# Tanh in place of SiLU in the routed expert tiles of a gated two-layer block, with ScalarE's order of work rewritten

## The chip, the cores and the metric

One core of a Trainium2 chip runs the whole program. The metric is the device time of one execution in microseconds (us). In what follows PE is TensorE, ACT is ScalarE, DVE is VectorE, POOL is GpSimd and SP is SyncE, which issues most of the DMA transfers.

## The reference

Two layers work on a residual stream `x` of 4 x 512 tokens with 512 channels, in fp32. Each layer adds a state-space block that reads a context (and is gated by `silu(layernorm(x))`), and then a feed-forward block. Layer 0's feed-forward block is a mixture of 16 experts, four of them chosen for each token, plus a shared expert. The part that the change touches is the experts' hidden layer:

```python
def body(acc, inp):
    g, u, d, we = inp
    y = jax.nn.silu(x @ g.T) * (x @ u.T) @ d.T
    return (acc + we[:, None] * y, None)
out, _ = jax.lax.scan(body, jnp.zeros_like(x), (gate_proj, up_proj, down_proj, cw.T))
```

`silu(a)` is `a * sigmoid(a)`, which is `0.5 * a * (1 + tanh(a / 2))`. The state-space block runs this recurrence over 512 time steps, for 512 channels with 16 states each:

```python
dA = jnp.exp(d_t[..., None] * A)
state = state * dA + (d_t * u_t)[..., None] * B_t[:, None, :]
y_t = jnp.einsum('ben,bn->be', state, C_t)
```

## The kernel before

The state-space blocks of the two layers and four sequences are eight stages `s` = 0 to 7. A stage has 32 units (16 states times two halves of the channels). For each unit ACT computes the decays, two activations with `Exp` (`decay`, L712); DVE multiplies `du` by the row of B (`mul_b`, L1702) and runs the scan (`scan`, L1710); POOL multiplies by the row of C (`mul_c`, L457), and the result is added up.

Stages 5 to 7 (`FIRST_B` is 5) run together with the routed experts of layer 0. The token rows are sorted by expert into 47 tiles: 32 whole ones of 256 rows and 15 half ones of 128 rows. From tile 4 on every third one is a half tile. Each of the 48 turns (16 in each of the three stages) holds two units of the recurrence and, in all but the first, one tile `j`. The engines walk the same turns, each in its own order written out by hand (`tile_turn` in each engine's block), and meet by semaphores.

For one tile PE transposes the gathered rows (`tile_transposes`, L1164), ACT copies them from PSUM to SBUF (`tile_rows`, L762), and PE multiplies them by the gate and up weights (`tile_in`, L1185), in two parts `it` = 0 and 1 that each end in one PSUM bank, `GU(j, it)`: the gate in its first half, the up product in its second. ACT applies the gate's function (`tile_silu`, L769), DVE multiplies by the up product (`tile_hidden`, L1728), and PE multiplies by the down weights (`tile_out`, L1196). ACT copies the result out (`tile_out`, L776) and SP stores it (`store_tile`, L341). The transposes of tile `j+1` are written into the banks of tile `j`'s gate and up products and so wait for its `tile_hidden`.

The weights of a tile are 1.5 MB and go into one of two slots (`load_tile_w`, L335). The load for tile `j+2` waits until PE is done with tile `j` (`y_done`). SP also loads, in each turn, a pair of B and C rows (`load_pair`, L316), which waits for POOL's `mulc_done`.

In 12 or so turns of stages 5 and 6 the engines also prepare the next stage (`prep`): PE's input projection (`in_one`, L1027), its projections L1058 and L1078, DVE's convolution (L1427), ACT's `conv_tap_one`, `silu_one` (which stays SiLU), `step_abs_one`, `exp_half`, `log_half` and so on.

Before the change ACT's order in a turn is: first decay of the turn, `tile_silu(j, 0)`, `tile_out(j - 1)`, `tile_silu(j, 1)`, `tile_rows(j + 1, 0)`, `tile_rows(j + 1, 1)`, second decay. DVE's order is: `tile_hidden(j, 0)`, `add_y`, `mul_b`, `tile_hidden(j, 1)`, `scan`, then `add_y`, `mul_b`, `scan` for the second unit, and the preparing work.

`ACT_TABLE_LOAD` rows are put ahead of an activation by the compiler where the function needs another table than the one loaded.

Of the kernel before, what the change touches and what calls it, by code (L numbers as in the profile page):

```python
# [69 lines left out]
def build(nc, t):  # L70
    with ExitStack() as ctx:
# [137 lines left out]
        y_done, yev, dve_step = sem("y_done"), sem("yev"), sem("dve_step")  # L209
# [326 lines left out]
        def _(act):  # L536
# [227 lines left out]
            def tile_silu(j, it):  # L764
                act.wait_ge(gu_done, j * 2 + it + 1)
                if j >= 2:
                    act.wait_ge(y_done, DONE[j - 1])
                n = P * BLOCKS[j]
                nc.scalar.activation(HT[:, j % 2, it, 0:n], GU(j, it)[:, 0:n], ACT.Silu).then_inc(sil_ready, 1)  # L769
# [141 lines left out]
            def tile_turn(s, i, prep):  # L911
                p = s + 1
                for u in range(BODY):
                    n = i * BODY + u
                    j = TPS * (s - FIRST_B) + n - 1
                    decay(s, i, 2 * u)
                    if prep:
                        if 2 <= n < 2 + ET:
                            conv_tap_one(p, n - 2)
                        if n == 10:  # L920
                            exp_half(p, 0)
                        if n == 13:
                            log_half(p, 0)

                    if j >= 0:
                        tile_silu(j, 0)
                    if j >= 1:
                        tile_out(j - 1)
                    if prep:
                        if n == 7:  # L930
                            x_dbl(p)
                        if n == 12:
                            plus_half(p, 1)
                        if n in (8, 9):
                            step_abs_one(p, 2 * (n - 8))
                    if j >= 0:
                        tile_silu(j, 1)
                    if prep and 3 <= n < 3 + ET:
                        silu_one(p, n - 3)
                    if 0 <= j < NTILE - 1:  # L940
                        tile_rows(j + 1, 0)
                    if prep:
                        if n == 11:
                            plus_half(p, 0)
                        if n in (8, 9):
                            step_abs_one(p, 2 * (n - 8) + 1)
                        if n == 14:
                            seed_half(p, 0)
                        if n == 15:
                            seed_half(p, 1)  # L950
                    if 0 <= j < NTILE - 1:
                        tile_rows(j + 1, 1)
                    decay(s, i, 2 * u + 1)
                    if s == FIRST_B and n == 0:
                        act.wait_ge(w_free, HS * FIRST_B + PRE_W)
                        nc.scalar.activation(flat(Y[:, 0, 2:4]), flat(PS[:, 0:2]), ACT.Copy).then_inc(y4_ready, 1)
                    if prep:
                        if n == 10:
                            exp_half(p, 1)
                        if n == 13:  # L960
                            log_half(p, 1)
# [5 lines left out]
            tile_out(NTILE - 1)  # L967
# [425 lines left out]
        def _(dve):  # L1393
# [130 lines left out]
            def route(b0, b1, work, rank1, rank2):  # L1524
# [59 lines left out]

                link(nc.vector.tensor_scalar(tot, tot, 2 * SCALING, TG[:, 2:3], ALU.mult, ALU.mult))
# [137 lines left out]
            def tile_hidden(j, it):  # L1723
# [3 lines left out]
                dve.wait_ge(sil_ready, j * 2 + it + 1)  # L1727
                nc.vector.tensor_tensor(h, h, GU(j, it)[:, TILE:TILE + n], ALU.mult).then_inc(h_ready, 1)  # L1728
# [362 lines left out]
```

## Time and profile before

| what | us |
|---|---|
| median of 3 runs | 1503.17 |
| lowest and highest run | 1501.42, 1510.47 |
| the profiled execution (its time) | 1501.42 |
| the profiled execution's span | 1499.7 |
| the stretch of the 47 expert tiles, from 788 to 1325 | 537.0 |

The span is the time from the first to the last instruction of the profiled execution; some 1.7 us of its time lie outside. The experts' tiles take 36% of it. Everything that the change touches lies in this stretch, apart from one constant in the routing.

### The profile page before, as it was taken

How to read it: one execution, taken by the hardware profiler on the slowest of the kernel's cores; microseconds unless marked ns; L12 is line 12 of the kernel's file. 1: busy time of each engine (PE TensorE's matmuls, PEld its weight loads, DVE VectorE, ACT ScalarE, POOL GpSimd, SP SyncE). 2: the span in 40 equal slices, each digit the busy share in tenths (PEclk: the TensorE clock that was granted, in tenths of full speed). 3: DMA queues.
4: the chain of work that ended last, by engine and by line, in shares of the span. 5: the costliest groups of instructions: out<-in, count | busy, mean ns of one | idle time of the engine just before them, and what ended most of it. 6: DMA issues, size and time to landing. Idle time of an engine off the chain costs nothing. (4 is left out here: it accounts for less than half of the span.)

```text
span 1499.7 us, 14543 instructions
## 1 busy us (share of the span) xinstructions
PE 1261.5 (84%) x4518; PEld 721.7 (48%) x4518; DVE 1353.0 (90%) x1319; ACT 971.4 (65%) x1528; POOL 784.2 (52%) x411
## 2 busy tenths in 40 slices
PE   7785796899699868996989998899988899826998
PEld 3331242443244324442556666566666666615555
DVE  4999999998999899988898988999899999888894
ACT  5766568575864666625866788767887767734442
POOL 0465566545555553550465555555565665565632
PEclk9799999999999998998899999999999999977999
DMA  7444545535544443450356678677777887755531
GB/s 254 109 141 127 126 141 142 154 98 151 133 146 124 127 127 109 126 154 2 99 181 233 239 260 291 230 272 239 254 275 230 286 273 273 270 183 147 167 100 57
DMA packets 99837, 264.31 MB, mean 176 GB/s; under 512 B 10832, under 2 KB 11344, under 8 KB 93616
## 3 DMA queue, kind: packets, MB, share of 16 engines
q1 hardware_dynamic: 87936, 225.36, 48.4%
q0 software_dynamic: 11440, 37.50, 7.7%
q8 instruction: 36, 0.59, 0.2%
q10 hardware_dynamic: 384, 0.52, 0.1%
q14 instruction: 41, 0.34, 0.1%
HBM read 233.73 MB, written 29.62 MB: 176 GB/s over the span
## 5 line engine op out<-in xcount | busy, mean ns | idle before, releaser
L457 POOL TENSOR_TENSOR state<-state,bc_rows 128x1024 f32<-128x1024 f32 x254 | 599.2, 2359 | 613.6 <-DVE banks L1702 613.5
L1095 PE MATMUL banks<-state,ident 128*128 128x512 f32 x640 | 323.7, 638 | 106.6 <-POOL state L457 106.6
L1710 DVE TENSOR_TENSOR_SCAN state<-decay,banks 128x1024 f32<-128x1024 f32 x176 | 402.0, 2284 | 11.4 <-DVE banks L1702 5.0
L1702 DVE TENSOR_TENSOR banks<-du,bc_rows 128x1024 f32<-128x1024 f32 x256 | 314.5, 1229 | 13.4 <-DVE state L1710 0.5
L1185 PE MATMUL banks<-z_gate,expert_w 128*128 128x256 f32 (+1 forms) x1504 | 284.1, 347 | 7.5 <-DMA expert_w<-in_moe_w 7.5
L1185 PEld LDWEIGHTS banks<-z_gate,expert_w 128*128 128x128 f32 x1504 | 248.8, 191 | 60.1 <-issue 18.9
L1095 PEld LDWEIGHTS banks<-state,ident 128*128 128x128 f32 x640 | 118.0, 197 | 282.0 <-POOL state L457 170.0
L712 ACT ACTIVATE decay<-delta,neg_a 128x511 f32<-128x511 f32 x352 | 226.4, 710 | 16.8 <-DVE state L1710 11.6
L1710 DVE TENSOR_TENSOR_SCAN state<-expert_w,banks 128x1024 f32<-128x1024 f32 x80 | 182.9, 2286 | 6.9 <-ACT expert_w L712 4.2
L1196 PE MATMUL banks<-expert_w,hidden 128*128 128x512 f32 x316 | 156.2, 610 | 2.3 <-ACT expert_out L776 1.2
L1721 DVE TENSOR_TENSOR y_scan<-y_scan,state 128x1024 f32<-128x1024 f32 x94 | 114.3, 1216 | 3.6 <-POOL state L457 2.0
L712 ACT ACTIVATE expert_w<-delta,neg_a 128x511 f32<-128x511 f32 x160 | 104.1, 711 | 8.5 <-DVE state L1710 6.9
L762 ACT ACTIVATE z_gate<-banks 128x512 f32<-128x512 f32 (+1 forms) x94 | 49.6, 529 | 76.1 <-PE banks L1164 75.5
L712 ACT ACT_TABLE_LOAD x65 | 83.4, 1283 | 1.6 <-ACT x_dbl L578 0.4
L769 ACT ACTIVATE hidden<-banks 128x256 f32<-128x256 f32 (+1 forms) x94 | 33.2, 353 | 61.3 <-PE banks L1185 60.8
L1196 PEld LDWEIGHTS banks<-expert_w,hidden 128*128 128x128 f32 x316 | 54.8, 198 | 34.5 <-issue 31.2
L1728 DVE TENSOR_TENSOR hidden<-hidden,banks 128x256 f32<-128x256 f32 (+1 forms) x94 | 35.1, 373 | 32.6 <-ACT hidden L769 31.9
L1144 PE MATMUL banks<-y_scan,expert_w 128*128 128x512 f32 x128 | 59.0, 615 | 5.0 <-DVE hidden L1736 5.0
L769 ACT ACT_TABLE_LOAD x47 | 60.3, 1283 | 0.8
L1046 PE MATMUL banks<-ones,ident 128*128 128x128 f32 x274 | 36.1, 290 | 28.4 <-DVE neg_mean_rstd L1933 28.4
L1353 PE MATMUL banks<-expert_w,du 128*128 128x512 f32 x128 | 55.6, 592 | 0.0
L1016 PE MATMUL banks<-ctx_t,in_w 128*128 128x512 f32 x96 | 47.3, 641 | 9.6 <-DMA ctx_t<-in_ctxT 7.3
(318 smaller groups left out, 1659.2 us busy)
## 6 DMA issues: line engine op xcount, KB each, us to landing
bc_rows<-bc_d SPq DMA_DIRECT2D x208, 512.0 KB
expert_w<-in_moe_w SPq DMA_DIRECT2D x48, 1536.0 KB, 9.1
ys_d<-expert_out SPq DMA_DIRECT2D x32, 512.0 KB, 5.4
ctx_t<-in_ctxT SPq DMA_DIRECT2D x8, 512.0 KB, 6.7
x_res<-in_x SPq DMA_DIRECT2D x4, 1024.0 KB, 10.7
xn_d<-y_scan SPq DMA_DIRECT2D x4, 1024.0 KB, 7.7
ys_d<-expert_out SPq DMA_DIRECT2D x15, 256.0 KB, 5.9
out_x<-x_res SPq DMA_DIRECT2D x3, 1024.0 KB, 6.0
```

The source lines that it names most:

```text
L457: nc.gpsimd.tensor_tensor(W[:, c % 4], W[:, c % 4], bcast2(BC[:, u, 1, :]), ALU.mult).then_inc(mulc_done, 1)
L712: ins = nc.scalar.activation(DAS[c % n][:, m, 1:], DEL[:, s % 2, et, 1:], ACT.Exp, scale=AN[:, lay(s), et, state:state + 1])
L762: nc.scalar.activation(XST[:, 2 * h:2 * h + 2, 0:n], XT(j)[:, h, :, 0:n], ACT.Copy).then_inc(xst_ready, 1)
L769: nc.scalar.activation(HT[:, j % 2, it, 0:n], GU(j, it)[:, 0:n], ACT.Silu).then_inc(sil_ready, 1)
L1095: mm = nc.tensor.matmul(PS[:, m], ID[:, :], W[:, c % 4, m, :], start=False, stop=True, skip_group_check=True)
L1144: mm = nc.tensor.matmul(AUX[g], MW[:, 0, at:at + P], XNT[:, k, :], start=(k == 0), stop=(k == ET - 1))
L1185: mm = nc.tensor.matmul(GU(j, it)[:, g * TILE:g * TILE + n], MW[:, u % 2, at:at + P], XST[:, k, 0:n], start=(k == 0), stop=(k == ET - 1))
L1196: mm = nc.tensor.matmul(out_bank(j, r), HT[:, u % 2, it, r * P:(r + 1) * P], MW[:, u % 2, at:at + D], start=(it == 0), stop=(it == IT - 1))
L1353: nc.tensor.matmul(PS[:, q], xnt[:, q, k * P:(k + 1) * P], BW[:, k, :], start=(k == 0), stop=(k == ET - 1))
L1702: nc.vector.tensor_tensor(drive(s), DU[:, s % 2, 2 * h:2 * h + 2, :], bcast2(BC[:, u, 0, :]), ALU.mult).then_inc(mulb_done, 1)
L1710: nc.vector.tensor_tensor_scan(flat(W[:, c % 4]), flat(DAS[c % da_slots(s, i)]), flat(drive(s)), 0.0, ALU.mult, ALU.add).then_inc(scan_don ...
L1721: nc.vector.tensor_tensor(y, y, W[:, k % 4], ALU.add).then_inc(w_free, 1)
```

## The change

The routed experts take `Tanh` with a scale of 0.5 in place of `Silu` (`tile_silu` becomes `tile_tanh`). DVE's `tile_hidden` gets one more instruction ahead of its product, `(tanh + 1) * gate`, which reads the gate from PSUM and writes to the same place in SBUF as before; a new semaphore `hg_ready` orders the two. What DVE has then is twice the SiLU product, and the routing weights are scaled by `SCALING` where it was `2 * SCALING` (the gate factor in `TG[:, 2:3]` holds a half already, which the shared expert, whose hidden layer is computed with `Tanh` before and after, needs).

ACT's order in a turn becomes: first decay, `tile_tanh(j, 0)`, second decay, `tile_tanh(j, 1)`, `tile_rows(j + 1, 0)`, `tile_rows(j + 1, 1)`, `tile_out(j)`. So the output of tile `j` is copied out at the end of its own turn, not in the next. The preparing work is spread anew between them: `silu_one`, for one, stood behind `tile_silu(j, 1)` and stands now between the second decay and `tile_tanh(j, 1)`. PE, POOL and SP keep their orders.

```diff
--- before.py
+++ after.py
@@ -206,7 +206,7 @@
 
         xt_done, xst_ready, gu_done, sil_ready, h_ready = (
             sem("xt_done"), sem("xst_ready"), sem("gu_done"), sem("sil_ready"), sem("h_ready"))
-        y_done, yev, dve_step = sem("y_done"), sem("yev"), sem("dve_step")
+        hg_ready, y_done, yev, dve_step = sem("hg_ready"), sem("y_done"), sem("yev"), sem("dve_step")
 
         rows_var, rows_std, rows_zn, rows_z = sem("rows_var"), sem("rows_std"), sem("rows_zn"), sem("rows_z")
         combined, exp_ready, shift_ready = sem("combined"), sem("exp_ready"), sem("shift_ready")
@@ -761,12 +761,12 @@
                 n = P * BLOCKS[j]
                 nc.scalar.activation(XST[:, 2 * h:2 * h + 2, 0:n], XT(j)[:, h, :, 0:n], ACT.Copy).then_inc(xst_ready, 1)
 
-            def tile_silu(j, it):
+            def tile_tanh(j, it):
                 act.wait_ge(gu_done, j * 2 + it + 1)
                 if j >= 2:
                     act.wait_ge(y_done, DONE[j - 1])
                 n = P * BLOCKS[j]
-                nc.scalar.activation(HT[:, j % 2, it, 0:n], GU(j, it)[:, 0:n], ACT.Silu).then_inc(sil_ready, 1)
+                nc.scalar.activation(HT[:, j % 2, it, 0:n], GU(j, it)[:, 0:n], ACT.Tanh, scale=0.5).then_inc(sil_ready, 1)
 
             def tile_out(j):
                 if j:
@@ -917,54 +917,51 @@
                     if prep:
                         if 2 <= n < 2 + ET:
                             conv_tap_one(p, n - 2)
-                        if n == 10:
-                            exp_half(p, 0)
-                        if n == 13:
-                            log_half(p, 0)
-
-                    if j >= 0:
-                        tile_silu(j, 0)
-                    if j >= 1:
-                        tile_out(j - 1)
-                    if prep:
                         if n == 7:
                             x_dbl(p)
                         if n == 12:
                             plus_half(p, 1)
-                        if n in (8, 9):
-                            step_abs_one(p, 2 * (n - 8))
                     if j >= 0:
-                        tile_silu(j, 1)
-                    if prep and 3 <= n < 3 + ET:
-                        silu_one(p, n - 3)
-                    if 0 <= j < NTILE - 1:
-                        tile_rows(j + 1, 0)
-                    if prep:
-                        if n == 11:
-                            plus_half(p, 0)
-                        if n in (8, 9):
-                            step_abs_one(p, 2 * (n - 8) + 1)
-                        if n == 14:
-                            seed_half(p, 0)
-                        if n == 15:
-                            seed_half(p, 1)
-                    if 0 <= j < NTILE - 1:
-                        tile_rows(j + 1, 1)
+                        tile_tanh(j, 0)
                     decay(s, i, 2 * u + 1)
                     if s == FIRST_B and n == 0:
                         act.wait_ge(w_free, HS * FIRST_B + PRE_W)
                         nc.scalar.activation(flat(Y[:, 0, 2:4]), flat(PS[:, 0:2]), ACT.Copy).then_inc(y4_ready, 1)
                     if prep:
+                        if 3 <= n < 3 + ET:
+                            silu_one(p, n - 3)
+                        if n in (8, 9):
+                            step_abs_one(p, 2 * (n - 8))
+                        if n == 10:
+                            exp_half(p, 0)
+                        if n == 11:
+                            plus_half(p, 0)
+                    if j >= 0:
+                        tile_tanh(j, 1)
+                    if 0 <= j < NTILE - 1:
+                        tile_rows(j + 1, 0)
+                    if prep:
+                        if n in (8, 9):
+                            step_abs_one(p, 2 * (n - 8) + 1)
                         if n == 10:
                             exp_half(p, 1)
                         if n == 13:
-                            log_half(p, 1)
+                            log_half(p, 0)
+                        if n == 15:
+                            seed_half(p, 1)
+                    if 0 <= j < NTILE - 1:
+                        tile_rows(j + 1, 1)
+                    if j >= 0:
+                        tile_out(j)
+                    if prep and n == 13:
+                        log_half(p, 1)
+                    if prep and n == 14:
+                        seed_half(p, 0)
 
             for s in range(FIRST_B, STAGES):
                 act.wait_ge(delta_ready, 2 * (s + 1))
                 for i in range(TURNS):
                     tile_turn(s, i, s + 1 < STAGES)
-            tile_out(NTILE - 1)
 
             act.wait_ge(ld_ffn1, 16 * 4)
             nc.scalar.activation(BB, BB, ACT.Copy, scale=TG[:, 3:4]).then_inc(bias_ready, 1)
@@ -1581,8 +1578,7 @@
                 link(nc.vector.reduce_sum(tot, cw, AX.X))
                 link(nc.vector.tensor_scalar(tot, tot, 1e-20, None, ALU.add))
                 link(nc.vector.reciprocal(tot, tot))
-
-                link(nc.vector.tensor_scalar(tot, tot, 2 * SCALING, TG[:, 2:3], ALU.mult, ALU.mult))
+                link(nc.vector.tensor_scalar(tot, tot, SCALING, TG[:, 2:3], ALU.mult, ALU.mult))
                 nc.vector.tensor_tensor(cw, cw, tot.unsqueeze(2).to_broadcast([P, nq, NE]), ALU.mult).then_inc(ranked, b1 - b0)
 
             def slots():
@@ -1725,6 +1721,9 @@
                 n = P * BLOCKS[j]
                 h = HT[:, j % 2, it, 0:n]
                 dve.wait_ge(sil_ready, j * 2 + it + 1)
+                nc.vector.scalar_tensor_tensor(out=h, in0=h, scalar=1.0, in1=GU(j, it)[:, 0:n], op0=ALU.add,
+                                               op1=ALU.mult).then_inc(hg_ready, 1)
+                dve.wait_ge(hg_ready, j * 2 + it + 1)
                 nc.vector.tensor_tensor(h, h, GU(j, it)[:, TILE:TILE + n], ALU.mult).then_inc(h_ready, 1)
 
             def shared_hidden(b, it):
```

## Rows read from the trace of the kernel before

**Rows 1.** The page: busy time of each engine over the whole span.

```profile
PE 1261.5 (84%) x4518; PEld 721.7 (48%) x4518; DVE 1353.0 (90%) x1319; ACT 971.4 (65%) x1528; POOL 784.2 (52%) x411
```

**Rows 2.** Windows, the expert-tile stage: busy time per engine, clock, DMA share, GB/s.

```profile
788.00:1325.00 537.00, 489.19 (x2186) 348.35 (x2184) 493.97 (x417) 400.56 (x606) 308.21 (x169) 0.98 0.75 255
```

**Rows 3.** Waits of DVE in that stretch: total us, times, longest.

```profile
DVE hidden L1728 <- ACT hidden L769: 31.9, 43, 2.1
DVE state L1710 <- DVE banks L1702: 5.0, 8, 0.6
```

**Rows 4.** Groups by line and shape, DVE, that stretch: busy, mean ns, idle before.

```profile
L1728 DVE TENSOR_TENSOR hidden<-hidden,banks 128x256 f32<-128x256 f32 x64 | 26.7, 417 | 26.6 <-ACT hidden L769 25.9
L1728 DVE TENSOR_TENSOR hidden<-hidden,banks 128x128 f32<-128x128 f32 x30 | 8.4, 281 | 6.0 <-ACT hidden L769 6.0
...
L1427 DVE SCALAR_TENSOR_TENSOR du<-banks,chan,du 128x511 f32<-128x511 f32 x8 | 5.8, 725 | 0.0
```

**Rows 5.** Groups by line, ACT, that stretch.

```profile
L712 ACT ACT_TABLE_LOAD x49 | 62.9, 1283 | 0.9
L769 ACT ACT_TABLE_LOAD x47 | 60.3, 1283 | 0.8
```

**Rows 6.** Timeline of ACT at a shared expert: start, duration, instruction.

```profile
294.51 0.60 ACT L755 ACTIVATE hidden<-banks 128x512 f32<-128x512 f32 x1 [2.30 <-PE banks L1144]
295.01 1.32 ACT L712 ACTIVATE expert_w<-delta,neg_a 128x511 f32<-128x511 f32 x2
```

**Rows 7.** Timeline of DVE at a shared expert.

```profile
700.68 0.69 DVE L1734 SCALAR_TENSOR_TENSOR hidden<-hidden,banks 128x512 f32<-128x512 f32 x1
701.41 0.69 DVE L1736 TENSOR_TENSOR hidden<-hidden,banks 128x512 f32<-128x512 f32 x1
```

**Rows 8.** Timeline across two turns, tile 45 (whole) to tile 46 (half).

```profile
1313.96 0.42 DVE L1728 TENSOR_TENSOR hidden<-hidden,banks 128x256 f32<-128x256 f32 x1
...
1314.30 2.28 DVE L1710 TENSOR_TENSOR_SCAN state<-decay,banks 128x1024 f32<-128x1024 f32 x1
...
1317.22 3.73 PE L1185 MATMUL banks<-z_gate,expert_w 128*128 128x128 f32 x32
...
1317.40 2.56 ACT L712 ACTIVATE decay<-delta,neg_a 128x511 f32<-128x511 f32 x4
...
1318.88 2.29 DVE L1710 TENSOR_TENSOR_SCAN state<-decay,banks 128x1024 f32<-128x1024 f32 x1
...
1319.98 1.28 ACT L769 ACT_TABLE_LOAD   x1
1321.27 0.28 ACT L769 ACTIVATE hidden<-banks 128x128 f32<-128x128 f32 x1
...
1321.58 0.29 DVE L1728 TENSOR_TENSOR hidden<-hidden,banks 128x128 f32<-128x128 f32 x1 [0.42 <-ACT hidden L769]
```

**Rows 9.** Chain that ended last, a whole tile: start, duration, instructions.

```profile
988.23 1.72 PE banks L1027 x4
...
1058.38 1.91 PE banks L1078 x4
...
1165.57 6.91 PE banks L1185 x32
1172.47 0.44 PE banks L1164 x4
1172.91 1.72 PE banks L1196 x4
```

**Rows 10.** The same chain where weights came last.

```profile
1230.54 11.89 DMA expert_w<-in_moe_w
...
1283.07 1.73 PE banks L1196 x4
1285.51 9.57 DMA expert_w<-in_moe_w
```

**Rows 11.** Timeline of the DMA issues on SP, the store behind that load.

```profile
1289.95 0.36 SPq L341 DMA_DIRECT2D ys_d<-expert_out  x1
```

## The prediction

> **What bounds the kernel now.** The page is read first: DVE is busy for 90% of the span, more than any other engine [rows 1]. The edits all act in the stretch of the expert tiles, so the windows view of that stretch is read next: of 537.0 us DVE is busy 494.0, PE 489.2 and ACT 400.6, at a granted clock of 0.98, and the DMA engines have a share of 0.75 [rows 2]. Two engines stand above 90%, and what matters is DVE's idle time, 537.0 - 494.0 = 43.0 us. The waits view says what ended it: 31.9 us, in 43 cases, by the activation that `tile_hidden` waits for (L769), and 5.0 us ahead of a scan [rows 3]. About 6 us more are spread.
>
> The timeline shows one such wait from end to end [rows 8]. DVE ends the product of tile 45 at 1314.38 (1313.96 + 0.42) and goes on without a stop to 1321.17, the end of the second scan, 6.8 us later. Meanwhile ACT runs four decays behind one table load (from 1317.40, 2.56 us), loads the other table (1319.98) and only then applies SiLU, at 1321.27. Its input had been there for some time: the PE began the gate and up products at 1317.22, and the first half of 3.73 us ends at 1319.1. DVE starts at 1321.58, with 0.42 us of idle time. So this wait is ACT's, and of table loads. Others are PE's, above all where it has extra work.
>
> **What the change removes.** SiLU and Exp alternate in every turn, at two table loads a turn: 49 ahead of decays and 47 ahead of SiLU, 123.2 us of ACT [rows 5]. With Tanh they go, if Tanh and Exp share a table. The trace bears that out: at a shared expert a Tanh at 294.51 is followed by decays at 295.01 with no load between [rows 6]. What stays in the stretch is the eight `silu_one`, with a load on each side (16 loads, 20.5 us), and about four for the logarithm. ACT falls from 400.6 us to about 400.6 - 123.2 + 20.5 = 298, 56% of the stretch. All of this lies on an engine with idle time; it is worth only what DVE and PE waited for it, at most 31.9 + 5.0 us.
>
> The page "ScalarE: Activation LUTs" of the Trainium skill (its section "What ACT_TABLE_LOAD costs") gives a switch as 1.283 us for the load and 1.38 us more to drain, 2.66 in all. The trace has only the first part: the load at 1319.98 ends at 1321.26 and the activation starts at 1321.27 [rows 8]. With the page's figure, as an estimate, the 96 loads would be worth 132 us more of ACT, and ACT would be as full as DVE.
>
> **What it adds.** DVE gets 94 instructions, 64 on 256 columns and 30 on 128. This instruction stands in the trace at the shared experts, on 512 columns: 0.69 us, and the product that waits for it starts 0.04 us after its end (700.68 + 0.69 = 701.37, next at 701.41) and takes 0.69 too [rows 7]. So it costs what the product costs, plus 0.04. The product takes 417 ns on 256 columns and 281 on 128 [rows 4]: 64 x 0.457 + 30 x 0.321 = 38.9 us. From below: an instruction that nothing waits for overlaps the next by 0.08 us (the scan at 1314.30 begins before 1314.38 [rows 8]); were that so here, 64 x 0.34 + 30 x 0.20 = 28 us. From above: the convolution's instruction of the same kind takes 725 ns on 511 columns [rows 4], 5% over 0.69, which gives about 41 us. I take 38.9, as the kind, the source bank and the wait are the same.
>
> All of it is on DVE, and nothing hides it but idle time. Where DVE no longer waits, one start in 43 cases moves back into the overlap: 43 x 0.08 = 3.4 us back. DVE's busy time becomes 494.0 + 38.9 - 3.4 = 529.5 us. With no idle time at all the stretch would shrink by 7.5 us; before, 43.0 were idle.
>
> **What idle time is left.** From the end of a tile's product (call it D) DVE reaches the next `tile_hidden` after 6.8 us. PE has then to do: the transposes and down products of the second half, 0.44 + 1.72 us, and half of the 6.91 us of the next gate and up products [rows 9] (the two rows of 0.44 and 1.72 come twice for a tile); a Tanh needs about 0.5 with its start. That is D + 0.05 + 2.16 + 3.46 + 0.5 = 6.2, so 0.6 us before it is wanted. A whole turn costs PE 6.91 + 2 x 2.16 = 11.2 us. For DVE, the 6.8 us hold two scans of 2.2 (each less its overlap) and `add_y` and `mul_b` once, so these take 2.4; its turn was 6.8 + 0.34 + 2.4 + 0.42, about 9.9, and becomes 10.8. A half tile costs PE about 6 (3.73 for the gate and up products [rows 8] and two halves of 2.16), and DVE 10.2. PE falls back by half a us in each of two whole tiles, and catches up in the half one. On plain turns DVE should not wait. The places where it should:
> - PE's extra work behind a whole tile where DVE has none: 1.72 us for an input projection, 1.91 for two of the other [rows 9]. Then the activation is at D + 8.1 against 6.8 and the second half late by 0.3: about 1.6 us each, at tiles 0, 5 and 23, together 5.
> - `silu_one` between the second decay and the second Tanh: two decays 1.4, load 1.3, SiLU 0.6, load 1.3 and the Tanh make the second Tanh late by about 0.7 in four or five of eight turns: 3. The mere order costs this; without it, nothing.
> - Weights. The load for tile j+2 is issued 0.7 us after PE's last product (1283.07 + 1.73, then 1285.51) and takes 9.57 there [rows 10]. For the whole tile behind a half one the chain is D + 2.2, 0.5 of PE's lag, 0.7, 9.6, 3.5, 0.5 = 17.0 us; DVE comes after 6.8 + 3.4 + 6.8 = 17.0, the middle term being its two products and what lies between them on a half tile (0.3 + 2.4 + 0.7). It is even at 9.6 us per load; some take 11.89 [rows 10]. I take 2 us over the 14 such places.
> - Starts and rests, POOL's lateness: 2 to 4.
>
> Together 13 us, give or take 5. The copy-out at the end of ACT's turn waits for PE (its end is D + 2.2), and behind it wait the next decay, which is ready by D + 4.4, and the Tanh, due at D + 5.7; the scan that needs the decay comes after two products, beyond D + 10. So this new wait costs nothing while PE keeps within 2 us or so of DVE, and if PE is later, DVE waits for PE anyway. SP's store of tile j-1 blocks `load_pair` for less time than before.
>
> **Sum.** 529.5 + 13 = 542.5 against 537.0: 5.5 us longer. Nothing else in the 1501.42 us of the profiled execution changes; one constant has the same price. That makes 1507. The median of the three runs lies 1.75 us above that execution, no more than runs differ by. I say 1506.
>
> **Rivals.**
> 1. *Balance* (the forecast): the loads' relief and DVE's new work are of one size. 1498 to 1514. For it: 38.9 us against 31.9 + 5.0 of waits. Against it: both are sums of small terms. Chance 0.70.
> 2. *All waits were ACT's.* If idle time falls to 4 us, 529.5 + 4 is 3.5 us less than 537.0, 1498; at the lower price of the instruction (28) it is 1487. For it: in rows 8 PE's result waited two us for ACT. Against it: PE's 11.2 us per whole tile and its extra work don't depend on ACT. (The switch of 2.66 us in the Trainium skill's page "ScalarE: Activation LUTs", section "What ACT_TABLE_LOAD costs", would end here: with it ACT would have set all 43 us.) Chance 0.15, of which 0.04 below 1488.
> 3. *The weights take over (slower).* The store of a tile is now issued right behind the load of the next weights, where before it came 4.4 us later (1285.51, then 1289.95) [rows 10, 11], and the rows for the transposes are gathered at the same time. If a load then lasts 11.9 us and not 9.6, each of the 14 whole tiles behind a half one is 2.3 us late: 32 us, 1538; it passes 1% at about 10.4 us per load, since 14 x 0.8 = 11 on top of the sum. For it: the 0.75 of DMA share and loads of 11.89 today. Against it: the bytes are the same, and the slower turns of DVE give the load more room. Chance 0.11.
> 4. *The rewritten order of ACT hurts elsewhere:* `x_dbl` and `plus_half` ahead of the first Tanh, the logarithm between the two `tile_rows`. They add 0.6 to 2.3 us each in some eight turns where ACT has over 1.5 us of room; if all of that lands on DVE, 10 us: 1517 or a bit more. Chance 0.04.
>
> **How the numbers follow.** Faster by over 1% is below 1488, slower by over 1% above 1518; about this much a measurement of this kernel can tell from no change. Faster: the 0.04 of rival 2. Slower: rival 3, half of rival 4 and 0.02 for the forecast's own terms being all too small, 0.15. Within 1%: 0.81. The range runs from 1494 (rival 2 with some idle time left) to 1520 (rival 3 at 10.5 us a load).
>
> **What the profile after would show.** Right: no table load at the decays of plain turns and some 20 in the stretch; ACT near 300 us there; DVE near 529 busy, the new instruction at 0.41 us on 256 columns with 0.04 to the product; DVE's waits for the Tanh below 12 us and at tiles 1, 6 and 24 or in the `silu_one` turns; loads of weights near 9.6. Wrong: loads over 10.4 us and PE's waits for `expert_w` grown (rival 3), DVE's idle time below 6 us (rival 2), or long waits at the turns of the logarithm (rival 4). The forecast falls if the added instruction is cheaper than 0.35 us, or if DVE's other instructions change their durations.

## The result and the profile after

The changed kernel takes 1515.38 us in the median of 8 runs (1514.14 to 1520.49), the kernel before, run beside it, 1508.26 us (1501.42 to 1513.34). The ratio is 1.0064, with a 95% interval of 1.0041 to 1.0087: the change costs some 10 us, and the table loads that it removes don't pay for it.

The two profiled executions differ by more, 1518.8 to 1499.7 us of span: the one before was the fastest of its eight runs, the one after 5 us slower than its median. The windows view of both, cut at the two ends of the expert tiles, tells where (columns: us; busy time and instructions of PE, weight loads, DVE, ACT, POOL; granted clock; DMA share; GB/s). Before, then after:

```profile
0.00:788.00 788.00, 645.12 (x1742) 290.83 (x1743) 723.86 (x624) 508.90 (x837) 385.61 (x174) 0.94 0.47 132
788.00:1325.00 537.00, 489.19 (x2186) 348.35 (x2184) 493.97 (x417) 400.56 (x606) 308.21 (x169) 0.98 0.75 255
1325.00:1499.70 174.70, 127.19 (x594) 82.52 (x592) 135.20 (x280) 61.99 (x86) 90.34 (x69) 0.89 0.44 133
```

```profile
0.00:796.87 796.87, 654.45 (x1742) 295.71 (x1743) 724.03 (x624) 508.94 (x837) 385.57 (x174) 0.94 0.49 131
796.87:1343.90 547.03, 489.87 (x2186) 346.87 (x2184) 525.42 (x511) 301.30 (x526) 312.57 (x169) 0.98 0.76 251
1343.90:1518.80 174.90, 127.20 (x594) 82.55 (x592) 135.16 (x280) 61.64 (x85) 89.86 (x69) 0.89 0.44 133
```

In the first stretch nothing of the program was changed and all engines but PE are busy for the same time, yet it lasts 788.0 us in one execution and 796.9 in the other. The kernels below show the same scatter: their first `tile_hidden` comes between 793.4 and 802.3 us. So each kernel is judged by its timed ratio, and the profiles by the stretch from the first start of `tile_hidden` to the last, which leaves the scatter ahead of it out. It is **530.7 us before and 540.6 after** (from starts read to 0.1 us), 9.9 us more, and the ratio says 9.7. Both measures have an error: the interval of a ratio is 3 to 4 us to either side, and a stretch is that of one execution. In some kernels below they differ by up to 6 us, and no run shows why; where it matters both are given.

Within the stage, ACT's groups by line after the change, which answer to [rows 5]:

```profile
L769 ACT ACTIVATE hidden<-banks 128x256 f32<-128x256 f32 (+1 forms) x94 | 32.4, 344 | 64.0 <-PE banks L1182 63.9
L712 ACT ACT_TABLE_LOAD x10 | 12.8, 1283 | 0.2
L571 ACT ACT_TABLE_LOAD x8 | 10.3, 1283 | 0.1
...
L627 ACT ACT_TABLE_LOAD x2 | 2.6, 1283 | 0.0
```

Of the 96 loads of [rows 5] 10 are left ahead of decays; with `silu_one` (L571) and the logarithm (L627) there are 20. ACT is busy 301.3 us where it was 400.6. DVE's groups by shape, which answer to [rows 4]:

```profile
L1727 DVE TENSOR_TENSOR hidden<-hidden,banks 128x256 f32<-128x256 f32 x64 | 26.9, 421 | 2.2
L1724 DVE SCALAR_TENSOR_TENSOR hidden<-hidden,banks 128x256 f32<-128x256 f32 x64 | 26.5, 414 | 12.3 <-ACT hidden L769 11.0 <-issue 0.9
L1727 DVE TENSOR_TENSOR hidden<-hidden,banks 128x128 f32<-128x128 f32 x30 | 8.6, 287 | 1.0
L1724 DVE SCALAR_TENSOR_TENSOR hidden<-hidden,banks 128x128 f32<-128x128 f32 x30 | 8.3, 275 | 0.2 <-ACT hidden L769 0.2
```

The new instruction (L1724) takes 414 and 275 ns, the product (L1727) 421 and 287. DVE is busy 525.4 us of 547.0 now, 494.0 of 537.0 before: 31 us more, and its idle time has halved, from 43.0 to 21.6. The waits view of the stage, which answers to [rows 3]:

```profile
ACT expert_out L776 <- DMA ys_d<-expert_out: 54.8, 28, 4.2
...
ACT decay L712 <- DVE state L1706: 33.6, 29, 3.2
...
ACT expert_out L776 <- PE banks L1193: 11.9, 33, 1.3
DVE hidden L1724 <- ACT hidden L769: 11.2, 21, 2.2
...
PE banks L1182 <- DMA expert_w<-in_moe_w: 6.7, 6, 1.7
...
DVE y_scan L1717 <- POOL state L457: 3.6, 7, 0.5
```

DVE's waits for the activation fell from 31.9 to 11.2 us. At the top ACT itself waits in two new ways: 54.8 us for the store of the tile before, and 33.6 for a scan. For the first the DMA view shows when the stores land (columns: KB of one transfer, median us from issue to landing); before, then after:

```profile
expert_w<-in_moe_w SPq DMA_DIRECT2D x45, 1536.0 KB, 9.1
...
ys_d<-expert_out SPq DMA_DIRECT2D x32, 512.0 KB, 5.4
```

```profile
expert_w<-in_moe_w SPq DMA_DIRECT2D x45, 1536.0 KB, 9.1
...
ys_d<-expert_out SPq DMA_DIRECT2D x32, 512.0 KB, 10.2
```

The store of a tile is issued right behind a load of weights (by 0.4 to 2.4 us in all turns but two, before by 3.8 to 8.3 in all but one) and lands after 10.2 us, where it took 5.4. The loads of weights have kept their 9.1. That it is the load ahead which delays the store is shown by a run below, `after_half_weights`: with the store as close behind a load of half the size, ACT's wait for it falls from 54.8 to 3.9 us.

### The profile page after: what moved, and what is told of

Read it like the earlier page. It is cut to its first block, busy times and chain, and to the rows that moved or that the text cites. A ratio compares the mean times of both kernels' runs of the same rounds, so it can differ in the third digit from the quotient of the medians.

```text
span 1518.8 us, 14557 instructions
## 1 busy us (share of the span) xinstructions
PE 1271.5 (84%) x4518; PEld 725.1 (48%) x4518; DVE 1384.6 (91%) x1413; ACT 871.9 (57%) x1448; POOL 788.0 (52%) x411
## 4 chain that ended last, share of the span: by engine, by line
DVE 35%; PE 30%; issue 8%; DMA 6%; POOL 5%; ACT 3%; DVEq 0%; SPq 0%; another core or an unknown queue 0%; ACTq 0%; POOLq 0%
DVE state L1706 15%; DVE banks L1698 10%; PE banks L1182 8%; PE banks L1092 5%; PE banks L1193 3%; DMA expert_w<-in_moe_w 3%; PE banks L1141 2%; DVE y_scan L1717 2%; POOL state L457 2%; PE banks L1036 2%; PE banks L1149 2%; DMA ys_d<-expert_out 1%; PE banks L1013 1%; DVE du L1424 1%; DVE hidden L1724 1%
## 5 line engine op out<-in xcount | busy, mean ns | idle before, releaser
L1092 PE MATMUL banks<-state,ident 128*128 128x512 f32 x640 | 328.3, 645 | 107.9 <-POOL state L457 107.6
L1706 DVE TENSOR_TENSOR_SCAN state<-decay,banks 128x1024 f32<-128x1024 f32 x176 | 402.1, 2285 | 10.2 <-ACT decay L712 5.8
L712 ACT ACTIVATE decay<-delta,neg_a 128x511 f32<-128x511 f32 x352 | 230.5, 712 | 48.5 <-DVE state L1706 43.7
L1717 DVE TENSOR_TENSOR y_scan<-y_scan,state 128x1024 f32<-128x1024 f32 x94 | 114.0, 1212 | 3.6 <-POOL state L457 3.6
L776 ACT ACTIVATE expert_out<-banks 128x512 f32<-128x512 f32 x79 | 45.5, 596 | 69.7 <-DMA ys_d<-expert_out 54.8
L472 POOL DMA_INDIRECT z_gate<-xn_d,selected x40 | 50.7, 1269 | 8.4 <-issue 5.3
L1043 PEld LDWEIGHTS banks<-ones,ident 128*128 128x128 f32 x274 | 35.2, 205 | 36.5 <-issue 36.5
## 6 DMA issues: line engine op xcount, KB each, us to landing
ys_d<-expert_out SPq DMA_DIRECT2D x32, 512.0 KB, 10.2
x_res<-in_x SPq DMA_DIRECT2D x4, 1024.0 KB, 10.8
```

Of the source, the lines that this page charges most:

```text
L712: ins = nc.scalar.activation(DAS[c % n][:, m, 1:], DEL[:, s % 2, et, 1:], ACT.Exp, scale=AN[:, lay(s), et, state:state + 1])
L1043: nc.tensor.matmul(bank[:, 0:P], ID[:, :], ON[:, :], start=True, stop=True)
L1092: mm = nc.tensor.matmul(PS[:, m], ID[:, :], W[:, c % 4, m, :], start=False, stop=True, skip_group_check=True)
L1706: nc.vector.tensor_tensor_scan(flat(W[:, c % 4]), flat(DAS[c % da_slots(s, i)]), flat(drive(s)), 0.0, ALU.mult, ALU.add).then_inc(scan_don ...
L1717: nc.vector.tensor_tensor(y, y, W[:, k % 4], ALU.add).then_inc(w_free, 1)
```

## Experiments

In the tables below "stretch" is the one just defined, from each kernel's profile; the last column is the time of three plain turns (a whole tile behind a half one, a whole one, a half one), the sum of the mean turn of each kind from the starts of the product in `tile_hidden` for tiles 32 to 45, where nothing is prepared. Ratios are to the kernel before, with their 95% intervals; "us by the ratio" is the ratio less 1, times 1508.26.

### Table loads and DVE's instruction taken apart

| kernel | table loads | DVE's instruction | ratio | us by the ratio | stretch | three turns |
|---|---|---|---|---|---|---|
| before | yes | no | 1 | 0 | 530.7 | 32.16 |
| `tanh_only` | no | no | 0.9939 (0.9919 to 0.9960) | -9.2 | 526.5 | 32.21 |
| `product_only` | yes | yes | 1.0117 (1.0096 to 1.0137) | +17.6 | 546.9 | 32.48 |
| `tanh_old_order` | no | yes | 1.0056 (1.0033 to 1.0080) | +8.4 | 540.7 | 32.69 |
| after | no | yes, new order | 1.0064 (1.0041 to 1.0087) | +9.7 | 540.6 | 32.73 |
| `after_no_product` | no | no, new order | 0.9961 (0.9937 to 0.9984) | -5.9 | 523.8 | 32.06 |

The expectations of this group count the stretch from the first to the last product of PE, on which the kernel before has 528.2 us and the changed one 537.6: some 3 us less than in the table.

**`tanh_only`.** One word changed in the kernel before:

```diff
-ACT.Silu).then_inc(sil_ready, 1)
+ACT.Tanh, scale=0.5).then_inc(sil_ready, 1)
```

> The kernel before with Tanh (scale 0.5) in place of Silu and nothing else: no factor gate*(1+..) on DVE, so the routed experts' values are not the reference's. It takes away the table loads alone. Theory A (whole tiles are set by PE's 11.2 us a turn, half tiles by DVE): the waits of DVE for the activation (31.9 us) mostly turn into waits for PE, so only about 10 us are gained: ratio 0.993, the stretch from the first to the last expert product 528.2 -> about 518 us. Rival B (the table loads were all that DVE waited for): -30 us, ratio 0.980, stretch 498.

The ratio is theory A's (9.2 us); of the stretch only 4.2 us came off, less than A's 10, and 3.3 of them before tile 15, where the next stage is prepared: three plain turns are no faster than before. Rival B is out. Its waits say why:

```profile
ACT hidden L769 <- PE banks L1185: 151.3, 81, 5.6
...
DVE hidden L1728 <- ACT hidden L769: 27.3, 32, 2.9
...
PE banks L1185 <- DMA expert_w<-in_moe_w: 10.0, 8, 2.2
```

Of the 96 table loads between decays and activations 12 are left, and DVE waits for the activation nearly as long as before (27.3 us, before 31.9). ACT itself waits 151.3 us for PE there, 60.8 before, and in all 32 of DVE's waits the Tanh had itself waited for PE. So where a table load had been the last to end, PE's work ended not much earlier, and took its place.

The trace of the kernel before shows it already, wait by wait. Of its 31.9 us, 18.1 (24 waits) stand behind a SiLU that had itself waited for PE, such as this one at tile 6, and 13.8 (19 waits) behind a SiLU that ran straight after its table load, as in [rows 8]:

```profile
870.58 0.38 ACT L769 ACTIVATE hidden<-banks 128x256 f32<-128x256 f32 x1 [1.63 <-PE banks L1185]
...
871.00 0.42 DVE L1728 TENSOR_TENSOR hidden<-hidden,banks 128x256 f32<-128x256 f32 x1 [0.75 <-ACT hidden L769]
```

At `tile_hidden` only those 13.8 us were ACT's own.

**`product_only`.** The other half of the change, added to the kernel before:

```diff
+nc.vector.scalar_tensor_tensor(out=h, in0=h, scalar=1.0, in1=GU(j, it)[:, 0:n], op0=ALU.add, op1=ALU.mult).then_inc(hg_ready, 1)
+dve.wait_ge(hg_ready, j * 2 + it + 1)
```

> The kernel before, SiLU and its table loads kept, with DVE's extra instruction (x+1)*gate added and waited for (the routed experts' values are then not the reference's). Theory A: DVE's 39 us lie to about two thirds in time in which DVE waited before, so +12 to +20 us, ratio 1.008 to 1.013, stretch 540 to 548; the waits for the activation fall from 31.9 to below 15 us although every table load is still there. Rival B (waits by the table loads stay, the work comes on top): +35 to +39 us, ratio 1.025.

The stretch grew by 16.2 us, in the range of A, and the ratio too. The waits:

```profile
DVE hidden L1728 <- ACT hidden L769: 19.0, 26, 2.1
...
PE banks L1185 <- DMA expert_w<-in_moe_w: 3.4, 4, 1.5
```

They fell by 13 us with every table load in place, to 19.0 and not below 15 as A had it; with the loads taken away alone they fell by 4.6. So most of the fall that the change shows comes from DVE being later, not from ACT being earlier.

**`tanh_old_order`.** The whole change but for ACT's order, which is that of before.

> Tanh, the extra DVE instruction and the routing constant as in the changed kernel, but ScalarE's order of the kernel before. Theory A: the order is worth next to nothing, time within 3 us of the changed kernel's (ratio to before 1.004 to 1.009, stretch 535 to 541). Rival C (the new order, with the copy-out at the end of the turn waiting for the store, costs): 6 us or more faster than the changed kernel, ratio at or below 1.002. Rival D (the new order is what kept the change from being worse): 6 us or more slower than it, ratio above 1.010.

The order is worth nothing that these runs can tell: 540.7 against 540.6 us, ratios 1.0056 and 1.0064. Rivals C and D are out. The 54.8 us that ACT waits for stores at the end of a turn lie in time that it has: of DVE's waits for the Tanh after the change, all but two (0.22 and 0.32 us) stand behind a Tanh that had itself waited for PE. The timeline after, at tile 37 (a half tile), shows how far:

```profile
1241.73 0.99 POOL L472 DMA_INDIRECT ctx_t<-xn_d,selected  x1
...
1243.02 1.98 POOL L472 DMA_INDIRECT ctx_t<-xn_d,selected  x1 [0.30 <-issue]
...
1244.41 0.29 DVE L1727 TENSOR_TENSOR hidden<-hidden,banks 128x128 f32<-128x128 f32 x1
...
1245.02 2.36 POOL L457 TENSOR_TENSOR state<-state,bc_rows 128x1024 f32<-128x1024 f32 x1
...
1247.41 1.23 DVE L1717 TENSOR_TENSOR y_scan<-y_scan,state 128x1024 f32<-128x1024 f32 x1 [0.51 <-POOL state L457]
...
1249.77 0.60 ACT L776 ACTIVATE expert_out<-banks 128x512 f32<-128x512 f32 x1 [3.66 <-DMA ys_d<-expert_out]
...
1250.27 1.32 ACT L712 ACTIVATE decay<-delta,neg_a 128x511 f32<-128x511 f32 x2
...
1251.49 0.37 ACT L769 ACTIVATE hidden<-banks 128x256 f32<-128x256 f32 x1
1252.02 0.40 DVE L1724 SCALAR_TENSOR_TENSOR hidden<-hidden,banks 128x256 f32<-128x256 f32 x1
```

DVE ends the half tile's second product at 1244.70. ACT copies the tile out only at 1249.77, after 3.66 us of waiting for the store; the decays and the Tanh follow, and that Tanh ends at 1251.86, 0.16 us before DVE comes for it at 1252.02. At this tile the wait costs nothing, with little to spare.

**`after_no_product`.** The changed kernel without DVE's instruction.

> The changed kernel without DVE's extra instruction (values of the routed experts not the reference's). Theory A: PE's 11.2 us per whole tile become the bound again; stretch 516 to 521 against 537.6 with the instruction, ratio to before 0.993; so 39 us of DVE work cost some 20. Rival B (DVE's 525 us busy is the bound by itself): the full 39 us come off, stretch 499, ratio 0.981.

16.8 us of the 39 come off (15.5 by the ratios), a little less than A's 20; A's 516 to 521 is 519 to 524 on this table's stretch, and 523.8 lies at its end. B is out. The prices, taken apart:

| what | by the stretch | by the ratios |
|---|---|---|
| the instruction, without table loads, old order | 14.2 | 17.6 |
| the instruction, with table loads | 16.2 | 17.6 |
| the instruction, new order | 16.8 | 15.5 |
| the table loads, without the instruction | 4.2 | 9.2 |
| the table loads, with it | 6.2 | 9.2 |

By either measure the instruction costs more than the loads did, and neither price shrinks when the other is there. How much the loads were worth, 4 or 9 us, stays open.

### Where the turn is bound

**`half_no_product` and `whole_no_product`.** The instruction left out in the half tiles only, or in the whole tiles only (there the condition is `KINDS[j]`, and in both the count waited for is fitted):

```diff
+                if not KINDS[j]:
+                    nc.vector.scalar_tensor_tensor(out=h, in0=h, scalar=1.0, in1=GU(j, it)[:, 0:n], op0=ALU.add,
+                                                   op1=ALU.mult).then_inc(hg_ready, 1)
+                    dve.wait_ge(hg_ready, 2 * (j - sum(KINDS[:j])) + it + 1)
-                nc.vector.scalar_tensor_tensor(out=h, in0=h, scalar=1.0, in1=GU(j, it)[:, 0:n], op0=ALU.add,
-                                               op1=ALU.mult).then_inc(hg_ready, 1)
-                dve.wait_ge(hg_ready, j * 2 + it + 1)
```

> The changed kernel with DVE's extra instruction left out in the 15 half tiles only (their values are not the reference's): 30 instructions, 9.6 us of DVE. Theory A (half tiles are DVE's, whole tiles PE's): nearly all of it comes off, stretch 540.6 -> 532 to 533.5, ratio to before about 1.001. Rival E (every turn shares the bound in the same proportion, 16.8 us for 39): 4 us, stretch 536.5.

> The changed kernel with the extra instruction left out in the 32 whole tiles only (their values are not the reference's): 64 instructions, 29.3 us of DVE. Theory A: only a third of it comes off, since PE's 11.2 us stand behind, stretch 530 to 532, ratio about 1.000. Rival E: 13 us, stretch 528, ratio 0.998. If DVE alone set the whole tiles: 29 us, stretch 511.

| kernel | us of DVE taken off | ratio | stretch | taken off the stretch | by the ratios |
|---|---|---|---|---|---|
| `half_no_product` | 9.6 | 1.0025 (1.0006 to 1.0043) | 538.5 | 2.1 | 5.9 |
| `whole_no_product` | 29.3 | 0.9978 (0.9956 to 1.0000) | 528.6 | 12.0 | 13.0 |

In the whole tiles both measures agree: DVE's work counts there, by 0.41 to 0.44 of it, as rival E's even share has it (13 us) and a little more than theory A had. For the half tiles they don't: 2.1 us by the stretch speak against theory A, which had nearly all of the 9.6 (E had 4), while by the ratios 5.9 come off, give or take some 4, which fits either. The waits of `half_no_product` name what stands behind DVE in its half turns, in which all ten waits for POOL lie:

```profile
PE banks L1182 <- DMA expert_w<-in_moe_w: 9.8, 9, 1.8
...
DVE y_scan L1717 <- POOL state L457: 8.6, 10, 1.0
```

`add_y` (L1717) waits 8.6 us for POOL where it waited 3.6 in the changed kernel, and PE waits 9.8 us for weights where it waited 6.7. In a half turn of the timeline above POOL issues two gathers (1241.73 and 1243.02, the second takes 1.98 us) ahead of its multiplication, which ends at 1247.38, and DVE's `add_y` stands 0.51 us for it. POOL and the weights come next there, not ACT: in the half tiles DVE waits for no Tanh.

**`mixed`.** SiLU in the half tiles, Tanh and the extra instruction in the whole ones:

```diff
+if KINDS[j]:
+    nc.scalar.activation(HT[:, j % 2, it, 0:n], GU(j, it)[:, 0:n], ACT.Silu).then_inc(sil_ready, 1)
+else:
     nc.scalar.activation(HT[:, j % 2, it, 0:n], GU(j, it)[:, 0:n], ACT.Tanh, scale=0.5).then_inc(sil_ready, 1)
```

The rest of the edit is not shown: in the half tiles DVE's product is one instruction with a factor of 2, and ACT's second decay stands behind `tile_rows(j + 1, 1)`.

> A version that computes what the reference does: Tanh and the extra instruction for whole tiles, SiLU without it for half tiles (their product takes a factor 2 in the same instruction), whose two table loads lie in turns where ScalarE has room; in a half turn the second decay stands behind the rows' copies. Theory A: about what half_no_product shows, stretch 532 to 535, ratio 1.000 to 1.004. Rival F: 30 table loads come back and set the half tiles as they did before (waits of 0.42 us each, 6 us), stretch 538 to 541, ratio about 1.006.

1.0058 (1.0038 to 1.0077), stretch 541.8: rival F's ratio, and a stretch 0.8 us beyond its range. It gave up the 2.1 us of `half_no_product` and more; DVE waited 6.0 us for SiLU in the half tiles, F's total, though in six waits and not in every half tile. The moved decay was not tried by itself.

**`after_two_products`.** The extra instruction done twice.

> The changed kernel with DVE's extra instruction done twice, each waited for (values of the routed experts not the reference's). 39 us more of DVE. Theory A: DVE now sets whole tiles as well, since 10.6 us + 0.9 pass PE's 11.2, so most of it counts: stretch 572 to 580, ratio 1.028 to 1.032. Rival G (DVE still hides behind PE or the weights as the first one did, at 16.8 for 39): stretch 557, ratio 1.018.

1.0230 (1.0201 to 1.0259), stretch 571.8, 31.2 us more for 39. By the ratios it is 25.0 us more. The ratio lies between A and G, the stretch at A's end. DVE is busy 554.0 of 571.8 us there. The first instruction cost 0.43 of its time, the second 0.80 (by the ratios 0.40 and 0.64): the cover is DVE's idle time, 43 us before, and half of it is used up after the change.

### What sets the floor without either

**`no_product_half_weights`, `after_half_weights`, `before_half_weights`.** Each load of weights from tile 2 on moves its first half only:

```diff
-                sp.dma_start(MW[:, slot, :], t["moe_w"][bass.ds(e, 1), :, :].rearrange("a p n -> p (a n)")
+                w = WPK // 2 if j >= 2 else WPK
+                sp.dma_start(MW[:, slot, 0:w], t["moe_w"][bass.ds(e, 1), :, 0:w].rearrange("a p n -> p (a n)")
```

> The changed kernel without DVE's extra instruction, and with each load of expert weights from tile 2 on cut to its first half, 0.75 MB for 1.5 MB, so that products use stale weights (values of the routed experts not the reference's). Before and the versions without the instruction all need about 32.1 us for three plain tiles, above PE's 28 and DVE's 29.4. Theory H (the loads of weights set that floor): three tiles fall to 29.5 to 30.5, stretch 523.8 -> 503 to 513. Rival P (POOL's late rows or another loop between the engines sets it): the stretch stays above 519.

> The changed kernel, its instruction kept, with the same halved loads of weights (values not the reference's). Theory H: DVE, now at 31.8 us for three plain tiles, stands close above the floor, so little comes off: stretch 540.6 -> 532 to 537, and the instruction, worth 16.8 us at full loads, is worth 24 us or more. Rival P: no change, 538 to 541, the instruction still worth 17.

> The kernel before, SiLU and table loads kept, with the same halved loads of weights (values not the reference's). Theory H: a part of the floor goes and ScalarE's chain of two table loads and four decays takes its place: stretch 530.7 -> 518 to 526, 8 us or more longer than the same without table loads (no_product_half_weights). Rival P: 528 to 531, and the table loads are worth no more than the 4 to 7 us seen at full loads.

| kernel | ratio, half loads | stretch, full loads | stretch, half loads | three turns, half loads |
|---|---|---|---|---|
| before | 0.9931 (0.9903 to 0.9960) | 530.7 | 526.2 | 31.17 |
| after | 1.0023 (0.9999 to 1.0047) | 540.6 | 537.0 | 32.03 |
| after, no extra instruction | 0.9909 (0.9879 to 0.9938) | 523.8 | 518.0 | 31.12 |

Halving the weights takes 3.6 to 5.8 us off the stretch (6.2 to 10.4 by the ratios). The floor of 32.1 us for three turns goes down to 31.1 and not to 29.5, so weights hold a part of it and something else the rest: without the instruction 518.0 us is neither theory H's 503 to 513 nor rival P's above 519. With short loads the instruction costs 19.0 us by the stretch and 17.2 by the ratios, not the 24 of H and hardly more than P's 17. The table loads with ACT's order are 8.2 us by the stretch, as H has it, but 3.3 by the ratios, so this isn't shown.

**`weights_first_before`.** The kernel before, with SP's `tile_turn` issuing the weights ahead of the B and C rows; only the order of issue is changed:

```diff
-                    if u == 0:
-                        load_pair(s, i, BODY - 1)
-                    elif i + 1 < TURNS:
-                        load_pair(s, i + 1, u - 1)
-                    elif s + 1 < STAGES:
-                        if u == 1:
-                            sp.wait_ge(bc_stored, 16 * (s + 2))
-                        load_pair(s + 1, 0, u - 1)
...
                     if m + 1 < NTILE:
                         load_tile_w(m + 1, (m + 1) % 2)
+                    if u == 0:
+                        load_pair(s, i, BODY - 1)
+                    elif i + 1 < TURNS:
+                        load_pair(s, i + 1, u - 1)
+                    elif s + 1 < STAGES:
+                        if u == 1:
+                            sp.wait_ge(bc_stored, 16 * (s + 2))
+                        load_pair(s + 1, 0, u - 1)
```

> The kernel before, with SP issuing in each turn the load of weights ahead of the load of B and C rows, so that it doesn't stand behind the wait for POOL; it computes the same. Theory H: in half turns the weights leave up to 1 us earlier, the wait of PE for weights (7.5 us) falls below 4 and the stretch falls from 530.7 to 523 to 528, ratio 0.995 to 0.998. Rival P: no change, ratio within 0.001 of 1.

0.9928 (0.9901 to 0.9955), 1497.25 us in the median: 11 us faster than before and faster than the changed kernel. The stretch is 522.9. Rival P is out, and the gain is larger than H's (0.995 to 0.998, 523 to 528). What the issuing queue of SP waited for in the stretch, before and then here:

```profile
SPq L341 <- ACT expert_out L776: 217.6, 45, 10.1
SPq L316 <- POOL state L457: 193.4, 42, 14.9
SPq L334 <- PE banks L1196: 29.7, 21, 6.5
```

```profile
SPq L334 <- PE banks L1196: 229.9, 45, 15.6
SPq L341 <- ACT expert_out L776: 200.1, 44, 10.1
SPq L316 <- POOL state L457: 2.2, 5, 0.4
```

SP stood 193.4 us in `load_pair` (L316), waiting for POOL, with the next load of weights behind it; now 2.2 us. PE's waits for weights, 7.5 us before, are gone from the waits view, and DVE's waits for the activation fell from 31.9 to 20.2 with every table load in place:

```profile
PE banks L1164 <- DVE hidden L1728: 39.8, 35, 4.8
...
DVE y_scan L1721 <- POOL state L457: 7.9, 12, 1.0
```

Three plain turns take 31.17 us, as with half the weights (31.17). So what the half loads brought in these turns can be had by the order alone, with all the bytes: what counted was when the weights arrive. The same order in the changed kernel wasn't run; there SP stood in `load_pair` for longer still, 379.4 us between 800 and 1325, where the kernel before has 178.4.

## Why the prediction was right, and where not

**The result** lies in the range and on the side of the forecast. The sum said 5.5 us for the stage; it was 9.9. Most of the way from the forecast 1506 to 1515.38 is not the change: the sum started from the profiled execution, 1501.42 us, which was the fastest of eight with a median of 1508.26. (The step from the sum's 1507 to 1506 has no term.)

- *Table loads:* "some 20 in the stretch", ACT at "about 298": 20 and 301.3. Right.
- *DVE's instruction:* 38.9 us was its price; 414 and 275 ns with 0.04 to the product are that. With the overlap given back DVE was to be busy 529.5 us, the gaps of 0.04 included; it is 525.4 and the gaps 3.2, so 528.6. Right.
- *Idle time left:* 13 us were forecast, "give or take 5", and 21.6 are there, of which 3.2 are those gaps: 18.4 against 13. This term is the miss. PE's extra work at tiles 1, 6 and 24 was named with their numbers, and there they are: 1.34 + 0.30, 1.67 + 0.30, 2.22 + 0.30 us, 6.1 against 5; two smaller ones at tiles 8 and 23 (1.17 each) were not. `silu_one` was put at 3 us; in three of its eight turns the second half lost the overlap of 0.1 us, and no more. What was left out: on plain whole tiles DVE's turn came out at 10.6 us where it doesn't wait and not at 10.8, against PE's 11.2, and in a dozen other places the Tanh came 0.2 to 0.5 us late, 3.6 us together; and POOL in half turns, another 3.6 us (seven waits of 0.51).
- *The new wait of ACT:* the forecast had ACT wait at the end of its turn for PE. It waits for PE 11.9 us and for the store 54.8: that `tile_out` also waits for the store of the tile before was not in the argument. The conclusion, that this costs nothing, holds (`tanh_old_order`), by the room that ACT has.
- *Rival 2* (all waits were ACT's) falls: DVE's idle time is 21.6 us and not 4, and in `tanh_only`, with 12 of the 96 loads left, the waits were still 27.3 us. In the trace 96 loads of 1.283 us, 123.2 us of ACT, were worth 4 to 6 us of the stretch and 9 by the ratios. The Trainium skill's page "ScalarE: Activation LUTs", section "What ACT_TABLE_LOAD costs", gives 2.66 us for a switch; as an estimate from it ACT would have been near full in the kernel before (400.6 + 132 of 537.0 us). The trace doesn't agree: the activation starts 0.01 us behind the load [rows 8].
- *Rival 3* (weights take over): the loads kept their 9.1 us, PE's waits for them went from 7.5 to 6.7. It did not occur in the change. Yet the weights were a bound in the kernel before, by the order in which SP issued them (`weights_first_before`), and in the changed one half loads took 3.6 us off the stretch.

The forecast itself was "the loads' relief and DVE's new work are of one size". That step was wrong: relief 4 to 9 us, new work 14 to 18, and not some 30 us of waits against 38.9 us of work. The 31.9 us of waits were read as mostly ended by table loads, because in [rows 8] one was; 18.1 of them were PE's, and they shrink with whatever makes DVE later, so that DVE's own new instructions used them as cover. The two errors meet in the same idle time and nearly cancel in the sum. That the total came out close is in this part luck.

What stays open: what holds three plain turns at 31.1 us once weights come early. POOL's 7.9 us of lateness in `weights_first_before` (2.0 before) speak for POOL's gathers; no run took them away. Nor did any run separate the clock or scatter of the first 790 us.

## What to carry to other kernels

A wait that ends with a slow instruction on another engine isn't that instruction's price: take the instruction away alone, and see whether the wait goes or only changes its last link. Look also at what the last link had itself waited for: that alone split the waits here into 18.1 us of PE's and 13.8 of ACT's. Where, as here, DVE and PE each fill about 90% of a stage, work taken from a third engine is worth little, and work added to the busiest costs a part of itself, 0.43 here for the first portion and 0.80 for the second (0.40 and 0.64 by the ratios). Before engines are relieved, look at what one engine that issues the transfers in order holds back behind a wait: two loads in the other order brought 8 to 11 us, where the exchange of functions cost 10.

## Not expected of the hardware

A store of 512 KB issued 0.4 to 2.4 us behind a load of 1.5 MB took 10.2 us to land (median), where the same store issued some 5 us behind it took 5.4; the load's own 9.1 us didn't change. Behind a load of 0.75 MB ACT's waits for the store fell from 54.8 to 3.9 us. POOL's issue of an indirect gather is of uneven length, 0.99 and 1.98 us for two in a row at tile 37, and there DVE waited for POOL behind it.
